# Two multi-head attentions written out batch by batch, with one product of each projection ahead of the weighted sums

## What is computed

```python
# layer 0, feed-forward part, its first half: two multi-head attentions, mixed by a router
n1 = _ln(x, ln1_g, ln1_b)                       # x is already normalised once by the caller
mha_probs = softmax(mean(n1, axis=1) @ mha_rw + mha_rb)
q, kk, v = n1 @ wq[m] + bq[m], n1 @ wk[m] + bk[m], n1 @ wv[m] + bv[m]    # m = 0, 1; 16 heads of 16
attn = softmax(q kk^T / 4);  ctx = attn v
x = x + sum_m (ctx @ wo[m] + bo[m]) * mha_probs[m]
n2 = _ln(x, ln2_g, ln2_b);  ffn_probs = softmax(mean(n2, axis=1) @ ffn_rw + ffn_rb)   # top 2 chosen

# layer 2, attention: 16 heads, keys masked by a padding mask
qp = (layernorm(x) @ Wq) * scale;  k, v = kv @ Wkv
attn = softmax(where(mask, lowest, qp k^T));  x = x + tanh(g) * ((attn v) @ Wproj + bproj)
```

## Time and profile before

| | us |
|---|---|
| median of 3 runs (3023.05 to 3033.63) | 3025.44 |
| the profiled execution | 3053.3 |
| its span, first to last instruction | 3051.6 |
| its mean granted TensorE clock | 0.954 of 2.4 GHz |
| `layer0_mha` in the span | 171.5 to 997.5 |
| `layer2_attention` in the span | 1751.7 to 2187.3 |

### The profile page before, as it was taken

One profiled execution on the slowest core, in us unless ns is written; L12 is line 12 of the kernel. 1 busy time (PEld: TensorE's weight loads), 2 busy tenths in 40 slices (PEclk: granted clock), 3 DMA queues, 4 the chain that ended last, 5 costly groups with the idle time before them and its releaser, 6 DMA issues. The chain is left out here.

```text
span 3051.6 us, 56496 instructions
## 1 busy us (share of the span) xinstructions
PE 2722.6 (89%) x19773; PEld 2165.8 (71%) x19774; DVE 1743.8 (57%) x4748; ACT 1143.3 (37%) x2188; POOL 627.0 (21%) x1027
## 2 busy tenths in 40 slices
PE   7978999989897899899899778888799998978998
PEld 6855666666665788787787645555588887877998
DVE  5757777777775111688675468888422217861111
ACT  1224444444443221454334424444333324452221
POOL 1211212121221000110464511111011104551111
PEclk9989999999998899999789979999799999988999
DMA  9610000000000443670214311000111102025553
GB/s 324 262 33 2 1 1 1 1 1 1 1 1 2 154 152 134 245 285 11 96 69 133 112 52 30 22 22 15 65 56 55 44 12 77 15 93 184 180 181 120
DMA packets 136169, 247.47 MB, mean 81 GB/s; under 512 B 26716, under 2 KB 86364, under 8 KB 129632
## 3 DMA queue, kind: packets, MB, share of 16 engines
q1 hardware_dynamic: 114608, 185.11, 18.0%
q10 hardware_dynamic: 11536, 35.28, 3.0%
q0 software_dynamic: 9888, 25.38, 2.3%
HBM read 148.75 MB, written 97.75 MB: 81 GB/s over the span
## 5 line engine op out<-in xcount | busy, mean ns | idle before, releaser
L564 ACT ACTIVATE m0hpT<-banks 128x1024 f32<-128x1024 f32 x256 | 262.9, 1027 | 415.3 <-PE banks L501 413.8
L539 DVE TENSOR_REDUCE m0hnm<-banks 128x4 f32<-128x1024 f32 x256 | 312.0, 1219 | 158.4 <-PE banks L488 156.9
L488 PE MATMUL banks<-m0hk,m0hq 32*128 32x256 f32 x2048 | 294.9, 406 | 71.4 <-DVE m0hnm L539 69.6
L501 PE MATMUL banks<-m0hq,m0hk 32*128 32x256 f32 x2048 | 294.3, 404 | 1.4 <-ACT m0hpT L564 1.4
L488 PEld LDWEIGHTS banks<-m0hk,m0hq 32*128 32x128 f32 x2048 | 177.4, 187 | 165.0 <-DVE m0hnm L539 142.4
L562 ACT ACTIVATE a2hpT<-banks,a2hlow 128x512 f32<-128x512 f32 x256 | 162.2, 684 | 208.0 <-PE banks L501 208.0
L539 DVE TENSOR_REDUCE a2hnm<-banks 128x4 f32<-128x1024 f32 x128 | 156.5, 1223 | 73.7 <-PE banks L488 73.6
L488 PE MATMUL banks<-a2hk,a2hq 32*128 32x256 f32 x1024 | 148.1, 407 | 44.6 <-DVE a2hnm L539 44.6
L501 PEld LDWEIGHTS banks<-m0hq,m0hk 32*128 32x128 f32 x2048 | 179.7, 186 | 3.2 <-issue 1.5
L488 PEld LDWEIGHTS banks<-a2hk,a2hq 32*128 32x128 f32 x1024 | 88.9, 187 | 98.0 <-DVE a2hnm L539 80.5
L3252 PEld LDWEIGHTS banks<-E3xT,E3w 128*128 128x128 f32 x1248 | 147.3, 194 | 2.4 <-DVE E3xT L3176 0.5
(11 more groups left out here) (492 smaller groups left out, 6219.9 us busy)
## 6 DMA issues: line engine op xcount, KB each, us to landing
E3w<-in_L_ffn_W_dram SPq DMA_DIRECT2D x39, 1024.0 KB, 4.8
slots<-A0pad SPq DMA_DIRECT2D x8, 4290.0 KB, 34.2
slots_x<-A1pad ACTq DMA_DIRECT2D x8, 4290.0 KB, 14.3
E0w<-in_L_ffn_fw_dram SPq DMA_DIRECT2D x64, 512.0 KB
E2w<-in_L_ffn_w_dram SPq DMA_DIRECT2D x16, 1024.0 KB
E1xin<-slots SPq DMA_DIRECT2D x71, 130.0 KB
m0hq<-m0hnmT SPq DMA_DIRECT2D x512, 1.0 KB
A2routed<-routed SPq DMA_DIRECT2D x16, 512.0 KB, 3.6
```

What stands on the lines that cost most here:

```text
L488: ins = pe.matmul(self.scores[:, j, tc], self.q[strip(half, j), u, e, c, chunk(tc)], self.k[strip(half, j), u, e, c], start=True, stop=True)
L501: ins = pe.matmul(self.turned[:, j, kc], self.k[strip(half, j), u2, e2, c2, chunk(kc)], self.q[strip(half, j), u2, e2, c2], start=True, st ...
L539: v.tensor_reduce(self.nm[:, e, :, at:at + 9:8].rearrange("p c g -> p g c"), self.scores, AX.X, ALU.max, negate=True).then_inc(self.nm_rdy, 1)
L564: ins = a.activation(dst, self.turned, ACT.Exp)
```

## The change

Both stages are written out batch by batch (B = 16) in place of the hardware loops, and `Heads` counts units from 0 to the end. In every call with a projection, TensorE's first product of it (2 of 8 instructions) stands ahead of the weighted sums, and the other three stand where `fill()` stood; in call 0 of `layer2_attention` the part ahead is the whole turn. The work between is spread anew:

- `layer0_mha`: the output sum becomes two halves (calls 4 and 7) in a PSUM bank of its own (bank 5), with four sets of turned-back outputs instead of two; v moves to calls 0 and 3, the turns to calls 3 and 4, the logits to calls 0 and 7. The two first norms become one: GpSimd takes both roots from one statistic, and ScalarE applies them. ScalarE also applies ln2 and copies q, in two halves around its exponentials, as k. The normalised residual is not kept but computed again by GpSimd in `make_base`. Sum, second norm and router of a batch come a batch later than its attention, the choice of experts another one.
- `layer2_attention`: GpSimd adds the routed rows and, ahead of time, the gated output bias; ScalarE applies the norm and copies q. The context and the mask column are read in place, without copies. The output projection has bank 5. SyncE loads the routed rows of four batches at the start and then one after the first unit's transfers of each batch.

```diff
@@ class Heads
-    def tensor(self, pe, job, u, i, first, fill=None):
...
-        if new:
-            score(1)
-        if old2:
-            score_turned(0)
-        if fill:
-            fill()
+    def tensor(self, pe, n, one=None, rest=None):
+        if self.has(n):
+            self.score(pe, n, 0)
+        if self.has(n - 2):
+            self.score_turned(pe, n - 2, 1)
+        if one:
+            one()
+        if self.has(n - 3):
+            self.weighted(pe, n - 3)
+        if self.has(n):
+            self.score(pe, n, 1)
+        if self.has(n - 2):
+            self.score_turned(pe, n - 2, 0)
+        if rest:
+            rest()
...
+def parted(pe, out, lhsT, rhs, ready, sem, after=None):
+    order = [(m, k) for m in range(C) for k in range(C)]
+    def step(m, k):
+        return pe.matmul(out(m), lhsT(k, m), rhs(k), start=(k == 0), stop=(k == C - 1))
+    def one():
+        ready()
+        step(*order[0])
+    def rest():
+        for m, k in order[1:]:
+            ins = step(m, k)
+        ins.then_inc(sem, 1)
+        if after:
+            after()
+    return one, rest
@@ layer0_mha, gpsimd
+            def norm1(b):
+                r = b % 4
+                g.wait_ge(st1_rdy, b + 1)
+                g.tensor_scalar(var1[:, r, 1], mv1[:, r, :, 1], 1.0 + 1e-6, 1e-11, ALU.mult, ALU.add)
+                ch1.link(g.tensor_tensor(var1[:, r, 0], mv1[:, r, :, 1], env.eps5[:], ALU.add))
+                ch1.link(g.tensor_tensor(root1[:, r].rearrange("p t c -> p (t c)"), var1[:, r].rearrange("p t c -> p (t c)"),
+                                         env.mhalf[:, 0:2 * C], ALU.pow))
+                for c in range(C):
+                    ins = g.tensor_scalar(shift1[:, r, c:c + 1], mv1[:, r, c, 0:1], root1[:, r, 1, c:c + 1], -1.0,
+                                          ALU.mult, ALU.mult)
+                ins.then_inc(rstd1_rdy, 1)
@@ layer0_mha, scalar
+            def take_q(job, e):
+                a.wait_ge(q_mm, job + 1)
+                for c in range(C):
+                    ins = a.activation(hd.q[:, job % 2, e, c], G0[:, c], ACT.Identity, bias=bqe[:, job % 2, e, c:c + 1],
+                                       scale=hd.column(2 + e))
...
+                hd.scalar(a, 8 * b, None, mid0)
+                hd.scalar(a, 8 * b + 1, pre1, mid1, end1)
+                hd.scalar(a, 8 * b + 2, own(take_q, 0), own(take_q, 1))
+                hd.scalar(a, 8 * b + 3, own(take_k, 0), own(take_k, 1), end3)
+                hd.scalar(a, 8 * b + 4, pre4, mid4)
+                hd.scalar(a, 8 * b + 5, None, mid5)
+                hd.scalar(a, 8 * b + 6, following(take_q, 0), following(take_q, 1))
+                hd.scalar(a, 8 * b + 7, following(take_k, 0), following(take_k, 1))
@@ layer0_mha, tensor
-            opened(pe, body, B)
+                if within(b):
+                    hd.tensor(pe, 8 * b, *make_v(0, ready0, after0))
+                    hd.tensor(pe, 8 * b + 1, *make_qk(wq, 1, G0, q_mm, ready1))
+                    hd.tensor(pe, 8 * b + 2, *make_qk(wk, 1, G1, k_mm, ready2))
+                    hd.tensor(pe, 8 * b + 3, *make_v(1, ready3, after3))
...
+                    hd.tensor(pe, 8 * b + 4, *sum_out(b - 1, 0, ready4, after4))
...
+                    hd.tensor(pe, 8 * b + 5, *make_qk(wq, 0, G0, q_mm, ready5))
+                    hd.tensor(pe, 8 * b + 6, *make_qk(wk, 0, G1, k_mm, ready6))
...
+                    hd.tensor(pe, 8 * b + 7, *sum_out(b - 1, 1, lambda: None, after7))
@@ layer2_attention, gpsimd (the adds were VectorE's) and tensor (one0 is the turn, rest0 the output projection)
+            def add_routed(b):
+                g.wait_ge(high_in[b % 2], 16 * (b // 2 + 1))
+                g.tensor_tensor(env.x[:, b], env.x[:, b], routed[:, b % 2, :, 0:D], ALU.add).then_inc(high_add, 1)
+                g.wait_ge(high_add, b + 1)
+                g.tensor_tensor(env.x[:, b], env.x[:, b], routed[:, b % 2, :, D:2 * D], ALU.add).then_inc(low_add, 1)
...
+                hd.tensor(pe, 4 * b, one0, rest0)
+                if more:
+                    hd.tensor(pe, 4 * b + 1, *make_q(b + 1, ready1))
+                    hd.tensor(pe, 4 * b + 2, *make_k(b + 1, ready2))
+                    hd.tensor(pe, 4 * b + 3, *make_v(b + 1, ready3))
```

More of the change, by code:

```diff
@@ L452, in __init__ @@
         self.qm_in = [sem_(tag + f"qm_in{i}") for i in range(4)]
[L453 removed]
+        self.put = 4 if low is None else 5
     def column(self, j):
@@ L532, in vector, with has @@
[L532 to L543 removed]
+    def has(self, n):
+        return 0 <= n < self.units
@@ L2272, in job @@
-            def job(b, u, first, last):
-                start, more = first and u == 0, not (last and u == 1)
-                ch.start(b + 2)
+            first_stats(0)
+            last_stats(0)
+            take_k(0, 0)
+            take_k(0, 1)
+            first_stats(1)
+            last_stats(1)
+            add_flags(1, 5).then_inc(low_rdy, 1)
+            v.wait_ge(low_rdy, 2)
+            v.wait_ge(hd.made, 3)
+            for b in range(B + 2):
+                more = b + 1 < B
                 def end0():
-                    if not start:
+                    if within(b - 1):
@@ L2386, in _ @@
+            one()
+            rest()
             turn(0, G1)
-            pe.wait_ge(q_in, 16)
-            make_q(0)
-            pe.wait_ge(w_in, 16 * loads)
-            make_v(0)
-            def job(b, u, first, last):
-                start, more = first and u == 0, not (last and u == 1)
-                def fill0():
+            pe.wait_ge(xnT_rdy, 1)
+            one, rest = make_q(0, lambda: pe.wait_ge(q_in, 16))
+            one()
+            rest()
+            pe.wait_ge(hd.q_rdy, 1)
```

1116 lines of the change are left out of this document (529 added, 587 removed).

## The result

The changed kernel takes 2910.14 us (median of 4 runs, 2905.0 to 2923.6), the kernel before 3024.24 us beside it: a ratio of 0.9623, 95% interval 0.9585 to 0.9661. The profiled execution took 2909.1 us round a span of 2907.4 us, at a mean granted clock of 0.964 of 2.4 GHz.

The account below looks back on a forecast made before the run. TensorE's in-order queue was taken as the bound. First attention 2.25 x 15.5 = 35 us, masked 1.2 x 15.25 = 18, less 3 for edges: 50 us off 3025.4, so 2975 us; forecast 2950 to 2995 (0.60), range 2944 to 3015.

Parts of the forecast that it names:

- The unstalled call: TensorE's call without a pause: 3.39 us plus filler, weighted sums 1.21 of it; 44.2 us a batch, 21.7 masked.
- Batches: Sign that the forecast is right: a batch takes 46.0 us in the first attention and 22.7 us in the masked one.
- The split's price: TensorE's projection in two parts around the weighted sums costs 0.20 us more, from candidates of 0.11, 0.20 or 0.41.
- rival of a full drain: TensorE empties at each split before taking the new shape, 0.41 us a split: 3011 us, chance 0.14.
- What it buys: Early product puts over 2.46 us of TensorE work between score pairs: the 0.16 us pause goes, VectorE gets slack.
- Work off VectorE: q, norms, statistics and adds leave VectorE: 7 of 37 us a batch, masked 4.4 of 19.3; pauses left 0.3 and 0.2.
- Onto ScalarE, GpSimd, SyncE: Moved work hides inside the loop: ScalarE 31 of 46 us a batch, GpSimd 14 of 46 and 8 of 22, SyncE 0.
- slower rival: ScalarE late in 77 q and k calls, each losing a 0.97 us half copy: 3050 us; with other losses, chance 0.13.
- Edges: Starts and ends of both stages: first attention -1.5, +2 and +1.3 us, masked +3 less 2; together +3 us.
- Clock dips: Dips to 1.2 GHz make some 0.5 and 0.24 us a batch; half of them go with fewer pauses.
- Unrolling: Four engines' loops become straight code: 0 to 6 us of waiting for issue possible, taken as 0.
- What would show it: Signs: L488's idle under 15 and 10 us, batch times, weighted sums 0.6 us after early product, VectorE near 70%, no gap.

Follow-up runs that it names:

- e1: Kernel before, with each of VectorE's maxima over half of the keys and the exponentials taking a sixteenth of the logits: 2954.12 us, ratio 0.9756.
- e5: Changed kernel with whole projections, maxima over half of the keys and exponentials over half of their columns: 2874.01 us, ratio 0.9487.
- e2: Changed kernel with maxima over half of the keys and exponentials of a sixteenth, the split product kept: 2905.97 us, ratio 0.9604.
- e4: Changed kernel with whole projections, maxima over half of the keys and exponentials of a sixteenth: 2939.05 us, ratio 0.9712.
- e10: Changed kernel with the copies of q in both stages and both norms' application in the first attention back on VectorE: 2920.94 us, ratio 0.9655.
- e13: As e10, but what VectorE did between a call's two maxima now stands behind the second: 3048.39 us, ratio 1.0076.
- e15: Changed kernel with VectorE's work between a call's two maxima moved behind the second, queries and norms left on ScalarE: 2948.63 us, ratio 0.9734.
- e6: Kernel before, with the projection's first product ahead of the weighted sums in 5 of 8 calls, 2 of 4 masked: 3014.94 us, ratio 0.9956.
- e3: Changed kernel with the single product moved back behind the second scores, so each projection is whole: 2959.86 us, ratio 0.9771.
- e14: As e13, with the projections whole: 3066.28 us, ratio 1.0126.
- e16: Kernel before with the edits of e6 and e1 together, single product and maxima over half of the keys: 2943.98 us, ratio 0.973.
- e7: Kernel before with its two attention loops written out, same instructions in the same order: 3022.15 us, ratio 0.998.
- e12: Changed kernel, first attention only: projections whole, and scores, maxima and exponentials handed over by PSUM bank: 2938.4 us, ratio 0.9719.

## Why the prediction was wrong

**The step that failed is "The unstalled call".** It took the weighted sums' 1.21 us from a stretch in which no pause is printed. The pair ahead of it started at 516.98, 2.47 us before the scores at 519.45: that is the 2.46 us that a maximum takes from scores to scores, which the next part of the prediction reads from the earlier trace rows. The 1.21 was the end of that wait:

```profile
516.98 0.48 PE L488 MATMUL banks<-m0hk,m0hq 32*128 32x256 f32 x2
...
518.16 1.23 DVE L539 TENSOR_REDUCE m0hnm<-banks 128x4 f32<-128x1024 f32 x1
```

The maximum ends at 519.39 and the scores start at 519.45. I set 2.46 against 1.09 + 1.21 = 2.30 and called 0.16 the pause; by e1 and e5 TensorE needs 1.09 + 1.00 = 2.09, and the pause is 0.37. The term was 0.21 too large in some 185 calls (8 x 15.5 + 4 x 15.25), 39 us of the 64 that the forecast lacks. The pauses of before were 5.5 us a batch and not 3.8, 2.8 and not 2.0 in the masked one (3.8 + 8 x 0.21, 2.0 + 4 x 0.21).

**Batches**: forecast 46.0 and 22.7 us, measured 43.9 and 21.7. Less the 1.7 and 0.8 us of that term the forecast stands at 44.3 and 21.9.

**The split's price** was right: 0.20 us by e2 against e5, 0.63 us from the early product to the weighted sums. The Trainium skill, TensorEngine Tiling (Array Packing), Key Properties, says that a change of tiling mode drains the engine; it gives no size, and by these runs the one change more in a call, with the second start of the projection, costs 0.20 us. The rival of a full drain (0.41) is out: the early product's 0.63 us and the rest's 1.49 make 2.12 for the 1.92 of the whole.

**What it buys** I had only half: two waits of like length lie on top of each other, VectorE's maxima for the scores (0.37 us) and ScalarE's exponentials for the turned ones (0.29 us; masked 0.4, a pair of 1.60 in e4 against 1.20 in e5). The prediction knew the first. The single product covers both, and e4 shows what covering one alone gives: 5.68 to 5.59 us.

**Work off VectorE** was the reason I gave for most of the pauses that go. The amount is worth about 11 us as long as the list is even (e10), and 100 when it is lumped (e13 less e15). What matters first is how it is laid: between two maxima the kernel before has pieces like this one, which starts behind the maximum of 503.56 in e6 (VectorE's list there is that of before):

```profile
503.56 1.23 DVE L541 TENSOR_REDUCE m0hnm<-banks 128x4 f32<-128x1024 f32 x1 [0.65 <-PE banks L488]
504.82 0.24 DVE L551 STREAM_TRANSPOSE m0hnmT<-m0hnm 128x64 f32<-128x64 f32 x1
...
506.15 0.29 DVE L846 TENSOR_SCALAR M0top<-M0top,M0ts,tg 128x2 f32<-128x2 f32 x1
506.59 0.17 DVE L847 COPY pick_w<-M0top 128x2 f32 x1
506.70 0.17 DVE L848 COPY pick<-M0ti 128x2 uint32 x1
507.02 1.23 DVE L541 TENSOR_REDUCE m0hnm<-banks 128x4 f32<-128x1024 f32 x1
```

3.46 us from maximum to maximum, VectorE never idle, for a choice of the two largest of eight numbers. The changed kernel cuts that into three pieces, each behind another maximum. Its own maxima, for the eye:

```profile
500.32 1.23 DVE L532 TENSOR_REDUCE m0hnm<-banks 128x4 f32<-128x1024 f32 x1
...
503.10 1.23 DVE L532 TENSOR_REDUCE m0hnm<-banks 128x4 f32<-128x1024 f32 x1 [0.58 <-PE banks L482]
...
505.62 1.23 DVE L532 TENSOR_REDUCE m0hnm<-banks 128x4 f32<-128x1024 f32 x1 [0.84 <-PE banks L482]
...
508.38 1.23 DVE L532 TENSOR_REDUCE m0hnm<-banks 128x4 f32<-128x1024 f32 x1 [1.21 <-PE banks L482]
```

Each step is 2.5 to 2.8 us, and VectorE waits in each. From the starts in the traces, the steps from a call's second maximum to the next call's first, in calls 0 to 7, means of the middle batches:

```
before    3.53 3.23 3.53 3.45 5.28 2.46 3.53 3.45
e6        3.53 3.23 3.53 3.45 5.28 2.42 3.53 3.02
after     2.92 2.51 2.58 3.08 2.96 2.58 2.57 2.93
e13       3.43 3.29 4.22 4.83 3.14 2.58 4.67 2.93
```

e6 has the steps of before but for the last, and what that gives back the step inside call 6 takes (2.92 us for 2.46): a split product shortens TensorE's side of a step that VectorE sets, and lengthens the other. That it gained nothing in the first attention (e6) and 50 us with an even list (e3 against after) fits this, and so do the 18 us it is worth with the lumps (e13 against e14). It is argued from the steps; the one run that was to show it by itself, e16, could not. So of the 114 us, 5 are the loops, some 60 the other rewriting (e7 to e3), and 50 the single product, and the last two are no independent parts. Of the rewriting the steps show this: from before to e3 the wait in W fell from 4.4 to 3.0 us a batch, in the masked stage from 2.9 to 1.3, some 45 us in all, which is VectorE's side; and P2 and P1 fell by 1.6 us a batch in the first attention, two thirds of it in calls 0 and 4, where the logits and the output sum had waited for ScalarE (L960). How much of VectorE's side is the even laying and how much the shorter list is not shown: no run undoes the laying alone.

**Output sum** (5.28 us in call 4 of before): cut in halves in a bank of its own, and the 5.6 us printed as its waiting for ScalarE are 0.0. I had counted them among the pauses and named no step for them; the same wait stood before the logits of call 0 (P2 of 1.56 us there, 1.64 in call 4).

**Onto ScalarE, GpSimd, SyncE**: right. TensorE's printed waits for the exponentials in the whole first attention are 1.4 us (turned scores) and 1.1 (weighted sums), the same as before, and no step of the table hides another, though ScalarE's busy time rose by 150 us. The slower rival (3050 us) had its condition, 4.0 of 5.5 us in one call, and not its effect.

**Edges**: forecast 3 us longer, measured 7 us shorter: the stages became 111 us shorter and the batches 104 of it (4.55 x 15.5 + 2.2 x 15.25). The masked stage's first scores came 26.3 us after its first weights (25.6 before), +0.7 and not +3: GpSimd's two shift instructions took 0.25 us each and not up to 0.65. Why the edges together came out shorter no run shows.

**Clock dips**: I halved them; in the stretches they are gone, 1.00 for 0.99, worth another 6 us at the 0.25 and 0.12 us a batch left in. **Unrolling**: 0 forecast, 5 gained.

**What would show it**: L488's idle under 15 and 10 us (6.4 and 3.0), weighted sums 0.6 us after the early product (0.63), VectorE's share near 70% (73%), no gap ahead of the weighted sums: all there. The one sign that came out otherwise is the batch, and it was the one that carries the time.

## What to carry to other kernels

Before you call a duration an engine's own, look whether the next instruction starts exactly one round trip of its partner after the one before: a wait shorter than the tail of the last product is not printed as idle. Where two engines alternate, even out what lies between the handovers, on both engines, before you shorten their lists; here moving queries and norms back to VectorE costs 11 us while its list is even, and the same work in lumps another 127. The two belong together: with that work on ScalarE the lumps cost 38. And when you remove one wait, name the second that ends at nearly the same time, for it will take the place.

## What was not expected of the hardware

- Splitting a projection of eight instructions around another product shape costs no more than 0.20 us: 5.49 against 5.30 us a unit (e2, e5).
- A hand-over of scores by PSUM bank gains nothing here: two maxima of about 690 ns fill 1.29 us against one of 1226 ns, so the second bank comes no earlier than both did, and the pair takes 1.51 us (e12).
- A VectorE operation on 128x8 elements took 0.23 us in the kernel before, 0.44 in e10 and 1.13 us in e13, there beginning 0.18 us behind a GpSimd operation of 1.28 us and ending with it, in 13 of 16 batches (e13, e14). The traces show that the two coincide; no run moves one of them alone.
- The way back from weighted sums to scores is 1.00 us in every run in which the maxima are early, so 0.31 us from the last start (1.00 less 0.69) and not the 0.52 us of the prediction. Into the weighted sums it was 0.31 us too, so both directions of that change cost the same.
